# Feed-forward attention: the split of queries and keys moves from VectorE to ScalarE and TensorE

## The reference

```
def _attn(x, wq, wk, wv, wo, bq, bk, bv, bo):
    q = (x @ wq + bq).reshape(Bb, T, H, hd).transpose(0, 2, 1, 3)
    k = (x @ wk + bk).reshape(Bb, T, H, hd).transpose(0, 2, 1, 3)
    v = (x @ wv + bv).reshape(Bb, T, H, hd).transpose(0, 2, 1, 3)
    att = jnp.einsum('bhqd,bhkd->bhqk', q, k) * hd ** (-0.5)
    att = jax.nn.softmax(jnp.where(causal, att, -jnp.inf), axis=-1)
    return jnp.einsum('bhqk,bhkd->bhqd', att, v)... @ wo + bo

for l in range(2):
    x = x + _attn(_ln(x), ...)
    x = x + moe(_ln(x), ...)      # l = 0: two of 8 experts per token; l = 1: two of 8 per sequence
```

## Time and profile before

| | |
|---|---|
| runs | 1312.77, 1309.41, 1305.33 us |
| the profiled execution | 1306.06 us, of which the span is 1304.4 us |
| TensorE (PE) busy | 1212.0 us, 93% |
| VectorE (DVE) busy | 926.4 us, 71% |
| ScalarE (ACT) busy | 804.6 us, 62% |
| GpSimd (POOL) busy | 711.3 us, 55% |

### The profile page before, as it was taken

How to read it: one execution, slowest core, us unless ns; L and a number is a source line. 1 busy time by engine, 2 the same in 40 slices (tenths; PEclk the granted TensorE clock), 3 DMA queues, 4 the chain that set the end, 5 groups by cost and what they waited for, 6 DMA issues and landing times.

```text
span 1304.4 us, 30732 instructions
## 1 busy us (share of the span) xinstructions
PE 1212.0 (93%) x9953; PEld 981.6 (75%) x9953; DVE 926.4 (71%) x2791; ACT 804.6 (62%) x1629; POOL 711.3 (55%) x1279
## 2 busy tenths in 40 slices
PE   4999999999998798999999999999999999999996
PEld 3777777777776577777776799998777777768996
DVE  7799999988776878888986222125888888635553
ACT  5677777666664366666666555564666666664552
POOL 4555555664331157777778531432677775446553
PEclk9999999999999999999999999999999999999999
DMA  4887887425666455454452688797656565356763
GB/s 120 227 240 233 228 226 188 127 79 144 177 170 158 116 133 127 125 139 129 121 132 61 213 234 235 240 259 225 152 150 150 158 153 147 83 159 178 213 200 103
DMA packets 208579, 216.93 MB, mean 166 GB/s; under 512 B 46691, under 2 KB 157795, under 8 KB 208420
## 3 DMA queue, kind: packets, MB, share of 16 engines
q1 hardware_dynamic: 191088, 193.49, 55.0%
q0 software_dynamic: 6304, 14.43, 3.7%
q10 hardware_dynamic: 11028, 7.06, 1.7%
HBM read 126.90 MB, written 85.46 MB: 163 GB/s over the span
## 4 chain that ended last, share of the span: by engine, by line
PE 59%; DVE 14%; SPq 7%; issue 6%; DMA 5%; POOL 4%; ACT 4%; POOLq 0%; DVEq 0%; ACTq 0%
PE weights L1600 6%; PE scores L640 5%; PE weights L697 4%; PE values L736 4%; DVE negmax L1041 4%; SPq L479 4%; PE weights L702 3%; PE values L743 3%; PE scores L1584 3%; PE scores L1861 3%; DMA windows<-parts 3%; PE scores L649 3%; PE weights L1877 3%; PE tokens L672 2%; SPq L461 2%
## 5 line engine op out<-in xcount | busy, mean ns | idle before, releaser
L1197 POOL TENSOR_SCALAR_AFFINE_SELECT probs<-probs 128x256 f32<-128x256 f32 (+1 forms) x576 | 280.8, 493 | 219.5 <-ACT probs L886 216.3
L886 ACT ACTIVATE probs<-weights 128x512 f32<-128x512 f32 x448 | 264.6, 597 | 109.0 <-PE weights L697 85.7
L1041 DVE TENSOR_REDUCE negmax<-scores 128x4 f32<-128x512 f32 x384 | 260.9, 685 | 76.0 <-PE scores L640 62.6
L640 PE MATMUL scores<-keys,queries 128*128 128x512 f32 (+1 forms) x384 | 182.2, 477 | 4.3 <-issue 0.8
L886 ACT ACTIVATE probs<-weights,keybias 128x512 f32<-128x512 f32 x192 | 131.5, 688 | 62.4 <-PE weights L697 47.5
L697 PE MATMUL weights<-queries,keys 104*128 104x256 f32 x768 | 156.4, 286 | 1.1 <-issue 0.9
L697 PEld LDWEIGHTS weights<-queries,keys 104*128 104x128 f32 x768 | 137.8, 191 | 21.6 <-issue 3.5
L1045 DVE TENSOR_REDUCE negmax<-scores 128x2 f32<-128x512 f32 (+1 forms) x192 | 130.9, 686 | 24.9 <-PE scores L646 15.4
L702 PEld LDWEIGHTS weights<-queries,keys 104*128 104x128 f32 x768 | 112.4, 191 | 10.7 <-ACT probs L886 0.9
L702 PE MATMUL weights<-queries,keys 104*128 104x128 f32 x768 | 108.1, 264 | 0.5 <-ACT probs L886 0.5
L736 PE MATMUL values<-probs,v 128*32 128x256 f32 x1536 | 104.4, 390 | 2.7 <-POOL probs L1197 2.7
(11 more groups left out here) (289 smaller groups left out, 2720.5 us busy)
## 6 DMA issues: line engine op xcount, KB each, us to landing
windows<-parts SPq DMA_DIRECT2D x192, 192.0 KB
queries<-windows SPq DMA_DIRECT2D x64, 384.0 KB
hidden_room<-in_m_w SPq DMA_DIRECT2D x78, 256.0 KB, 3.1
out_room<-in_m_w SPq DMA_DIRECT2D x78, 256.0 KB, 3.2
keys<-windows SPq DMA_DIRECT2D x192, 96.0 KB
routed_rows<-zeros SPq DMA_DIRECT2D x64, 256.0 KB, 3.5
windows<-parts SPq DMA_DIRECT2D x64, 120.0 KB
expert_rows<-probs ACTq DMA_DIRECT2D x46, 128.0 KB
```

The costliest lines, as they stand in the source:

```text
L640: i = pe.matmul(bank[:], queries[0:rows, s, t * P:(t + 1) * P], keys[0:rows, s::S4, half * P:(half + 1) * P], start=True, stop=True)
L886: act.activation(probs[:, n % RING], weight_banks[n % 2][:], ACT.Exp, scale=SCALE, **bias).then_inc(exp_done.sem, 1)
L1041: i = dve.tensor_reduce(most[:, part, s, :], bank[:].rearrange("p (a k) -> p a k", k=P), AX.X, ALU.max, negate=True)
L1197: pool.affine_select(out=block, in_=block, compare_op=ALU.is_ge, fill=0.0, base=0, pattern=[[0, heads], [1, P]], channel_multiplier=-1).th ...
```

## The change

For ffn items ScalarE writes the high parts straight from the bank `tokens` into `W[:, 0]` (two activations with bias). TensorE then multiplies them with a negative identity and accumulates the product onto the projections in the bank, which leaves value minus high part. ScalarE reads the bank a second time with the same biases and writes the low parts. VectorE's two instructions go for these items, as does `QK`. The bank is released by the second reading. A new constant `minus_ident` is made by GpSimd in the set-up.

```
-        ident_r = const("ident_r", [P, P], F32R)
+        ident_r, minus_ident = const("ident_r", [P, P], F32R), const("minus_ident", [P, P], F32R)
...
-            pe.matmul(X[:, 0:T], U.wq[:], src[:], start=True, stop=True)
+            pe.matmul(X[:, 0:T], U.wq[:], src[:], start=True, stop=U.kind != "ffn", skip_group_check=U.kind == "ffn")
...
-            tokens_bank.until(qk_taken.sem, qk_taken.at(g))
+            if U.kind == "ffn":
+                if not 3 * B <= g < 3 * B + LANES:
+                    yield
+                pe.wait_ge(high_ready.sem, high_ready.at(g))
+                pe.matmul(X[:], minus_ident[:], W[:, 0], start=False, stop=True, skip_group_check=U.kind == "ffn").then_inc(high_taken.sem, 1)
+                tokens_bank.until(split_ready.sem, split_ready.at(g))
+            else:
+                tokens_bank.until(qk_taken.sem, qk_taken.at(g))
...
         def act_project(act, g):
             X, U = tokens, units[g]
             act.wait_ge(projected.sem, projected.at(g))
+            if U.kind == "ffn":
+                for n in (1, 2) if units[g - 1].kind == "ctx" else (1,):
+                    act.wait_ge(windows_stored.sem(g - n), windows_stored.at(g - n))
+                act.wait_ge(high_copied.sem, high_copied.at(g - 1))
+                act.activation(W[:, 0, 0:T], X[:, 0:T], ACT.Identity, bias=U.bq[:])
+                act.activation(W[:, 0, T:2 * T], X[:, T:2 * T], ACT.Identity, bias=U.bk[:]).then_inc(high_ready.sem, 1)
+                yield from rest(0 if 3 * B <= g < 3 * B + LANES else 2)
+                act.wait_ge(high_taken.sem, high_taken.at(g))
+                act.activation(W[:, 1, 0:T], X[:, 0:T], ACT.Identity, bias=U.bq[:])
+                act.activation(W[:, 2, T:2 * T], X[:, T:2 * T], ACT.Identity, bias=U.bk[:]).then_inc(split_ready.sem, 1)
+                yield
+                return
...
         def dve_split(dve, g):
             U = units[g]
+            if U.kind == "ffn":
+                return
...
+            done(pool.memset(minus_ident[:].bitcast(F32), 0.0))
             wait()
             select(ident_r[:], ALU.not_equal, 1.0, [[-1, P]])
+            select(minus_ident[:], ALU.not_equal, -1.0, [[-1, P]])
```

More of the change, by code:

```diff
@@ L354, in decoder @@
         transposed, src_ready = signal("transposed"), signal("src_ready")
-        projected, qk_taken = signal("projected"), signal("qk_taken")
+        projected, qk_taken = signal("projected"), signal("qk_taken", {"self": 1, "ctx": 1})
+        high_taken = signal("high_taken", {"ffn": 1})
         high_ready, split_ready, high_copied = signal("high_ready"), signal("split_ready"), signal("high_copied")
@@ L579, in pe_project @@
             else:
-                i = pe.matmul(X[:, T:2 * T], U.wk[:], src[:], start=True, stop=U.kind != "self")
+                i = pe.matmul(X[:, T:2 * T], U.wk[:], src[:], start=U.kind != "ffn", stop=False, skip_group_check=U.kind == "ffn")
                 if U.kind == "self":
@@ L834, in act_project @@
                 act.activation(QK[:, 0:T], X[:, 0:T], func, bias=U.bq[:])
[L835 to L838, removed]
+                i = act.activation(QK[:, T:2 * T], X[:, T:2 * T], func)
             i.then_inc(qk_taken.sem, 1)
```

## The result

The changed kernel takes 1346.4 us (median of 4 runs, 1344.1 to 1348.9), beside 1307.9 us of the kernel before (4 runs, 1305.3 to 1312.8). The ratio is 1.030, with a 95% interval of 1.027 to 1.032. The forecast was 1345.5 us, slower by 36 us; the medians differ by 38.5 us. The profiled execution of after took 1344.1 us, of which the span is 1342.2 us.

What follows compares the result with a forecast made beforehand. TensorE was taken to set the pace, with VectorE late only in part of layer 0's chain. Terms 20.6 (layer 0's routed items) + 3.6 + 7.8 + 4.0 = 36 us on the 1309.4 median gave 1345.5 us, range 1324 to 1360.

Steps and rivals of the forecast that it cites:

- (a): VectorE's two removed instructions, 32 times: worth 0 in layer 0, at most TensorE's 0.15 us wait per item in layer 1.
- (b): TensorE's product in slot -15: 0.46 us waiting for both high parts plus 0.25 us of product, 0.71 us per item.
- (d): Layer 0, VectorE's L1051 and GpSimd's mask come apart: 0.3 us back per routed item, between 0 and 0.44.
- (c): Slot -14, layer 0: L780 waits for ScalarE's second pair to free the bank, 1.46 us per item in 11 items.
- (e): First five items of layer 0: 3.6 us lost in sum, 2 of it at the first item's moved transfer wait.
- (f): Layer 1, 13 steady items: 0.71 less 0.15, about 0.6 us each, 7.8 us; the later second pair costs nothing.
- (g): First three items of layer 1: TensorE waits for the high parts and runs the product, 1.3 us each, 4.0 us.
- the one in which only the product costs: Rival: the routing stage's wait is covered, (c) falls to 0.4 at most; 1332 us, down to 1324; chance 0.14.
- The one in which delays add up: Rival: later pair delays layer 1's transfers 0.6 us per item, routed items lose another 0.7; 1361 us; chance 0.11.
- The one in which VectorE is the late engine: Rival: relief of VectorE gains up to 0.7 us in 29 items, some 20 us: 1289 us; chance 0.04.

Runs made afterwards that it cites:

- kernel without either wait: Against the changed kernel, ScalarE's second pair goes ahead of `aoT` and the product becomes its own stage in slot -14: 1311.1 us, ratio to before 1.003.

## Why the prediction was right, and its one wrong step

- **(a) VectorE's instructions: 0.** Right, and this carries the sign. The kernel without either wait, in which TensorE could have used any relief, gained at most 0.3 us per item in layer 0 and lost the product's time in layer 1. Not even the 0.15 us of layer 1 came back by VectorE's relief: in after L680 waits for VectorE 0.2 us in all, where L672 waited 1.4, but in the kernel without the waits it is 1.4 again. In after TensorE comes later by itself, and that covers the wait.
- **(b) The product: 0.71 forecast, 0.76 measured**, in both layers, by the kernel without it. The second high part ends at 584.42 + 0.47 = 584.89, and the product starts at 584.94: a hand-over of 0.05, as taken from the earlier trace rows. The bracket has only 0.30 for the wait, as TensorE's ends are modelled. By the starts it is the 0.46 of the forecast: in before the next scores start 0.43 us after ScalarE's first reading, in after the product starts 0.89 after it. From there to the next start are 0.34 us (585.28), where I had 0.25; that makes 0.80 in this item, and 0.76 by the periods. The wait is the larger part: free of it the product costs 0.29 us in layer 1 and in layer 0 no more than (d) returns.
- **(c) The bank in slot -14: 1.46 forecast, 1.39 in the bracket.** By the starts it is 1.55: ScalarE ran in the order foretold, and L788 started 1.82 us after L771, where it was 0.27; I had said 1.7. That it is the order on ScalarE, and not the reading of the bank, is shown by the pair ahead of `aoT`, which takes 1.25 us back.
- **(d) 0.3 back.** L1070 lasts 0.17 in place of 0.61, and 0.14 of that is lost again at L1079. The chain's way on VectorE, from L1060 to TensorE's taking of the tokens, is 9.53 us (589.60 to 599.13) in place of 9.67 (580.59 to 590.26), and 9.88 in the item before that one: 0.14 to 0.35 back. So 0.3 is within what was measured, at its upper end. The rule on the shared read port in the Trainium skill, SBUF — State Buffer (section "SBUF: two separate sides"), under which the two engines hold each other up only while they overlap, agrees with the shorter L1070; that it was the overlap that went was not tried by itself.
- **(e) 3.6 forecast, 3.4 in the timed runs**, though the interval is wide (1.0 to 5.6), and the 3.6 was itself added up from guesses with bounds of several us, so that it came this close is luck. The part with the transfer went as told: the first item's wait has moved from VectorE to ScalarE, and TensorE, at its product, waits 2.17 us for ScalarE. But VectorE doesn't run free, as I had written: it is idle for 4.96 us, until its scores come at 409.02.

```profile
405.97 0.47 ACT L840 ACTIVATE parts<-tokens,l_bq 128x256 fp32r<-128x256 f32 x1 [2.82 <-DMA windows<-parts]
```
- **(f) Layer 1: 0.6 forecast per item, 1.15 measured.** This is the step that failed: "The second pair stands ahead of an exponential, about 0.8 us later than now, with a slot and more before its room is needed." It asks only when the room is needed, not who waits for that exponential. The order was seen, and its follower was not: GpSimd's mask, and behind it on GpSimd a row of masks and indirect transfers with hardly a gap. That is 0.39 us per item, 4.2 us in all (202.9 to 198.7 with the pair a slot later). The rest of the miss is the 0.05 in (b) and the 0.15 that I took off in full: the wait for VectorE is gone from L680, but there TensorE now waits for ScalarE (`queries`, L884), 2.4 us in 11 items where it was 0.7 in 2. The transfers behaved as foretold: the parts go out 4.67 us after the first reading (1065.31 in SyncE's queue) in place of 3.26, 1.4 later, and nobody waits for them.
- **(g) 4.0 forecast, 4.3 measured**, and gone in the kernel that leaves the three alone.
- **The sum.** With layer 0's 20.0 or 18.0, the first five's 3.4, 13.1 for the steady items of layer 1 (12 distances) and 4.3 for its first three, the measured parts add up to 40.8 or 38.8 us, beside the 38.5 of the medians (35.6 to 42.1 from the ratio). They agree within what both are uncertain by. The forecast of 36 came so close partly by luck: layer 0 was put 0.6 to 2.6 us too high, and layer 1's steady items 5 us too low.

Of the rivals, the one in which only the product costs falls with the 1.39 us at L788. The one in which delays add up had half of the right mechanism, an exponential that is late for its follower; but in layer 1 it gave the 0.6 us per item to late transfers, for which nobody waits, where the late exponential costs 0.39, and of its 0.7 more in layer 0 nothing was seen. The one in which VectorE is the late engine was tried in its own conditions and gave nothing that the steady items show. The busy share of 90% that spoke for it was work that kept pace with TensorE: in after the stretch from 560 to 580 us has VectorE busy for 15.11 of 20 us and TensorE for 16.39.

## What to carry to other kernels

Taking work off an engine pays only where that engine is the last to arrive; here both engines were busy for about 90% of a stretch or more, and the chain and one idle gap of 0.31 us told which of them was late. When an intermediate result goes through another engine and back, price the two hand-overs and the place of the answer in the other engine's queue: the product cost 0.3 us at most, and its two waits 1.9. For every instruction that is put ahead of another in an in-order queue, look up who waits for the second one, and whether that engine has a gap in which it can catch up.

## What the runs showed of the hardware

VectorE's busy time fell by 43 us, not by 35. Beside L1070, the pre-norm's output in layer 1 (L964, L947 before) became shorter, though it is the same pair of instructions. In before, GpSimd had begun to issue an indirect transfer 0.33 us before VectorE's pair; in after it began 0.35 us behind its start. VectorE and GpSimd in before:

```profile
1025.27 1.44 DVE L947 TENSOR_SCALAR tok<-xin,meanvar_pre,rstd_pre 128x128 f32<-128x128 f32 x2
```
```profile
1024.94 1.01 POOL L1290 DMA_INDIRECT table<-expert_rows,y_index  x1 [0.17 <-issue]
```

and in after:

```profile
1071.44 0.61 DVE L964 TENSOR_SCALAR tok<-xin,meanvar_pre,rstd_pre 128x128 f32<-128x128 f32 x2
```
```profile
1071.79 1.01 POOL L1309 DMA_INDIRECT out_room<-expert_rows,y_index  x1 [0.17 <-issue]
```

So 0.83 us of the pair's busy time was, as far as the rows tell, a wait within the instructions. Over all 64 of them the mean went from 543 (516 in the second profile) to 424 ns and stayed at 429 without the product. It was 513 again in the kernel with neither wait, whose items have nearly the old length, but also 543 with the pair a slot later in layer 1, whose items are 0.8 us longer than before; there GpSimd's issue again starts 0.30 us before VectorE's pair (1073.35 and 1073.65). So it hangs on how the two engines' queues lie against each other. The Trainium skill, SBUF — State Buffer (section "Who interferes with whom"), says that whichever of VectorE, in a mode that uses two ports, and GpSimd starts first keeps the shared ports for its whole instruction. VectorE's times in both orders above agree with it; on GpSimd's side no wait shows, as its issue lasts 1.01 us in either order. It bought nothing: a shorter entry in the busy time is no shorter kernel when the engine isn't late.
